# Graph-attention layer front end: norm weight and bias applied as the turned tile leaves PSUM, loads in another order, half of the first accumulator cleared by GpSimd in the front

## The reference

```python
def _gat_conv(x, edge_index, W, att_src, att_dst, bias, heads, out_ch, concat):
    ...
    h = (x @ W).reshape(n, heads, out_ch)
    a_src = jnp.sum(h * att_src[None], axis=-1)
    a_dst = jnp.sum(h * att_dst[None], axis=-1)
    e = jax.nn.leaky_relu(a_src[src] + a_dst[dst], NEG_SLOPE)
    ...
    out = jax.ops.segment_sum(h[src] * alpha[..., None], dst, num_segments=n)
    ...
mu = jnp.mean(x, axis=-1, keepdims=True)
var = jnp.var(x, axis=-1, keepdims=True)
h = (x - mu) / jnp.sqrt(var + LN_EPS) * ln_w + ln_b
h = jax.nn.elu(_gat_conv(h, edge_index, W1, att_src1, att_dst1, b1, H1, C1, True))
return _gat_conv(h, edge_index, W2, att_src2, att_dst2, b2, 1, D, False)
```

## Time and profile before

| | us |
|---|---|
| median of 3 runs | 3159.04 (3158.66 to 3159.12) |
| the profiled execution | 3158.56 |
| its span, first to last instruction | 3156.7 |
| front, to the last `rows` (L519) | 0 to 135.2 |
| first gather of the first walk | 138.86 |
| first walk's gathers | 880, L785, 871.0 busy |
| busy over the span: PE, DVE, POOL, ACT | 2642.0, 2378.1, 1829.8, 1356.0 |

### The profile page before, as it was taken

How to read it: one execution, slowest core, us unless ns; L and a number is a source line. 1 busy time by engine, 2 the same in 40 slices (tenths; PEclk the granted TensorE clock), 3 DMA queues, 4 the chain that set the end, 5 groups by cost and what they waited for, 6 DMA issues and landing times. The chain is left out here.

```text
span 3156.7 us, 72672 instructions
## 1 busy us (share of the span) xinstructions
PE 2642.0 (84%) x16531; PEld 2040.5 (65%) x16532; DVE 2378.1 (75%) x7838; ACT 1356.0 (43%) x5016; POOL 1829.8 (58%) x1892
## 2 busy tenths in 40 slices
PE   6789889888888988796888877877778774999997
PEld 5667767776776777684666665655555554666675
DVE  5699889889988988876777666777888763446465
ACT  3456656665665655342333322444444224221211
POOL 0167777777777777205777777777777735011111
PEclk9889999999999999897999998889989865999999
DMA  6467777777777777214555936333343435232320
GB/s 187 146 195 222 221 215 225 220 223 216 222 222 215 209 209 208 81 56 122 159 154 151 317 106 188 106 106 105 106 106 105 106 106 193 89 102 74 123 73 9
DMA packets 217462, 489.43 MB, mean 155 GB/s; under 512 B 47565, under 2 KB 97241, under 8 KB 217258
## 3 DMA queue, kind: packets, MB, share of 16 engines
q0 software_dynamic: 119696, 367.15, 41.5%
q1 hardware_dynamic: 82782, 106.04, 10.5%
q10 hardware_dynamic: 14780, 13.93, 1.4%
HBM read 427.70 MB, written 64.16 MB: 156 GB/s over the span
## 5 line engine op out<-in xcount | busy, mean ns | idle before, releaser
L1286 POOL DMA_INDIRECT weights<-table,w_idx x880 | 843.1, 958 | 403.9 <-issue 245.6
L785 POOL DMA_INDIRECT w_G<-table,w_idx x880 | 871.0, 990 | 347.8 <-issue 255.6
L918 PE MATMUL PS<-w_G,w_S 128*128 128x260 f32 x3520 | 885.2, 394 | 130.9 <-DVE ACC L1010 112.4
L918 PEld LDWEIGHTS PS<-w_G,w_S 128*128 128x128 f32 x3520 | 637.3, 191 | 236.3 <-issue 86.3
L1493 PE MATMUL PS<-weights 128*128 128x257 f32 x1760 | 530.9, 432 | 141.3 <-DVE ACC L1690 71.8
L1493 PEld LDWEIGHTS PS<-weights 128*128 128x128 f32 x1760 | 336.0, 211 | 251.7 <-issue 154.9
L998 DVE TENSOR_TENSOR w_G<-w_G 128x512 f32<-128x512 f32 x660 | 436.8, 690 | 31.3 <-ACT w_G L815 19.1
L826 ACT ACTIVATE w_G<-w_G 128x64 f32<-128x64 f32 x1760 | 441.3, 335 | 0.0
L1314 ACT ACTIVATE w_PW<-w_Z 128x4 f32<-128x4 f32 x220 | 45.2, 205 | 694.5 <-DVE w_Z L1675 694.3
L1010 DVE TENSOR_TENSOR ACC<-ACC,PS 128x520 f32 x464 | 320.4, 690 | 15.9 <-PE PS L918 15.9
L2397 POOL DMA_INDIRECT out<-Oe,who x64 | 62.3, 973 | 414.8 <-DVEq L2449 408.1
(11 more groups left out here) (333 smaller groups left out, 3799.5 us busy)
## 6 DMA issues: line engine op xcount, KB each, us to landing
xbuf<-XR SPq DMA_DIRECT2D x8, 2064.0 KB
weights<-in_L_ffn_w SPq DMA_DIRECT2D x16, 1024.0 KB, 8.5
XB<-xbuf SPq DMA_DIRECT2D x7, 2064.0 KB, 8.7
w_G<-table,w_idx POOLq DMA_INDIRECT x880
weights<-table,w_idx POOLq DMA_INDIRECT x880
table<-row SPq DMA_DIRECT2D x49, 260.0 KB, 2.0
xw_wide_path<-table SPq DMA_DIRECT2D x49, 260.0 KB, 4.0
table<-row ACTq DMA_DIRECT2D x49, 129.0 KB, 2.2
```

The costliest lines, as they stand in the source:

```text
L785: pool.indirect_dma_start(G[:, r, b, :], None, table, IndexOn(ap=idx[:, r, b:b + 1], axis=0)).then_inc(fetched[r], 16)
L918: last = pe.matmul(PS[:, 2 * j + a, 0:W // layer.banks], lhsT, rhs, start=b == slots[0], stop=b == slots[-1])
L1286: pool.indirect_dma_start(G[:, r, b, :], None, table, IndexOn(ap=idx[:, r, b:b + 1], axis=0)).then_inc(fetched[r], 16)
```

## The change

It does six things.

1. BA, `bias`, its four matmuls and `weights` are gone. `copy(t)` is now two ACTIVATEs of 128x128 (one per half), each with the norm's bias and weight as per-partition operands; it waits once for their load (`norm_in`). `rows(t)` copies instead of adding BA.
2. The two att loads stand on SP's queue behind the first piece of x, and no longer on ACT's behind W1.
3. PIECES are 4, 9, 14 and 22. The first four tiles are normalised, turned and copied ahead of `tile(0)`. `attention` is cut in two, with `scales(0)` between its halves.
4. DVE's side work stands at other tiles: `statistics` of the second piece behind `rows(0)` too, `scales` of the third and fourth piece behind `rows(9)` and `rows(23)`, `crossings` behind `rows(24)` (before, `rows(13)`).
5. xt is no tile of its own. It lies in the part of ACC from tile 24 on, so ACC is there from the front on.
6. POOL clears ACC's tiles 0 to 23 in the front, in one memset behind its two fetches for `crossings`; the memset of DVE in the walk is gone, and ACT clears tiles 24 to 48.

```diff
-PIECES = (4, 13, 16, 16)
+PIECES = (4, 9, 14, 22)
+BLANKED = 24
...
-        xt = sb("xt", [P, TILES, D])
+        xt = ACC[:, BLANKED:, :].rearrange("p t c -> p (t c)")[:, 0:TILES * D].rearrange("p (t d) -> p t d", d=D)
...
             piece(0)
+            for j, v in enumerate((dev["att_s1"], dev["att_d1"])):
+                sp.dma_start(att[:, j, :], v.rearrange("h c -> (h c)").partition_broadcast(P)).then_inc(w1_in, 16)
...
                                         IndexOn(ap=slot_i[:, 0:1], axis=0)).then_inc(across_in, 16)
+            pool.memset(ACC[:, 0:BLANKED, :], 0.0)
...
-                act.activation(YT[:, t % 4, :, :], PS[:, 4 + t % 2, 0:2 * P].rearrange("p (k q) -> p k q", k=2), ACT.Copy).then_inc(y_copied, 1)
+                for k in range(2):
+                    last = act.activation(YT[:, t % 4, k, :], PS[:, 4 + t % 2, k * P:(k + 1) * P], ACT.Identity, bias=lb[:, k:k + 1], scale=lw[:, k:k + 1])
+                last.then_inc(y_copied, 1)
...
-                dve.tensor_tensor(row[:, r, :].rearrange("p (a b) -> p a b", a=2), PS[:, 2 * u:2 * u + 2, 0:HALF],
-                                  BA[:, 0:ROW1].rearrange("p (a b) -> p a b", a=2), ALU.add)
-                dve.tensor_tensor(AD1[:, t, :], PS[:, 2 * u + 1, HALF:HALF + 16], BA[:, ROW1:ROW1 + 16], ALU.add).then_inc(rows_ready, 1)
+                dve.tensor_copy(row[:, r, :].rearrange("p (a b) -> p a b", a=2), PS[:, 2 * u:2 * u + 2, 0:HALF])
+                dve.tensor_copy(AD1[:, t, :], PS[:, 2 * u + 1, HALF:HALF + 16]).then_inc(rows_ready, 1)
...
+            def some(t, first, per, p):
+                a = FROM[p] + per * (t - first)
+                if first <= t and a < FROM[p + 1]:
+                    statistics(p, range(a, min(a + per, FROM[p + 1])))
+
-            statistics(0, range(0, 4))
+            statistics(0, range(0, FROM[1]))
             spread(0)
-            attention()
+            attention(0)
             scales(0)
-            bias()
-            statistics(1, range(4, 17))
-            weights()
+            attention(1)
+            statistics(1, range(FROM[1], FROM[1] + 5))
             for t in range(TILES):
+                if t == 1:
+                    statistics(1, range(FROM[1] + 5, FROM[2]))
+                    spread(1)
                 rows(t)
...
+                some(t, 0, 2, 2)
+                some(t, 10, 2, 3)
+                if t in (7, 21):
+                    spread((7, 21).index(t) + 2)
+                if t in (9, 23):
+                    scales((9, 23).index(t) + 2)
+                if t == 24:
                     crossings()
...
-            dve.memset(ACC[:, 0:HALFWAY, :], 0.0).then_inc(zeroed, 1)
-            dve.wait_ge(zeroed, 1 + -(-(TILES - HALFWAY) // 4))
+            dve.wait_ge(zeroed, -(-(TILES - BLANKED) // 4))
```

More of the change, by code:

```diff
@@ L242, in gps_program @@
             ACC = sb1("ACC1", [P, TILES, ROW1])
+            dev.update(W2A=W2A, b1c=b1c, b1m=b1m, AD1=AD1)
+            front(nc, allocator, dev, ACC)
             walk(nc, allocator, dev, LAYER1, table1, AD1, ADM, SELF, ACC)
@@ L263, in gps_program, with front @@
         return dev
-PIECES = (4, 13, 16, 16)
-def front(nc, allocator, dev):
+PIECES = (4, 9, 14, 22)
+BLANKED = 24
+def front(nc, allocator, dev, ACC):
     PS, ident, iota_row, ones, mean, rstd, unit, SRC, DST, TK, AD1 = (dev[k] for k in (
@@ L388, in copy @@
                     act.wait_ge(tile_done, t - 3)
-                act.activation(YT[:, t % 4, :, :], PS[:, 4 + t % 2, 0:2 * P].rearrange("p (k q) -> p k q", k=2), ACT.Copy).then_inc(y_copied, 1)
+                for k in range(2):
+                    last = act.activation(YT[:, t % 4, k, :], PS[:, 4 + t % 2, k * P:(k + 1) * P], ACT.Identity, bias=lb[:, k:k + 1], scale=lw[:, k:k + 1])
+                last.then_inc(y_copied, 1)
             root(0)
-            normal(0)
-            normal(1)
-            for t in range(TILES):
+            for t in range(FROM[1]):
+                normal(t)
+            act.wait_ge(norm_in, 2 * 16)
+            for t in range(FROM[1]):
+                copy(t)
+            root(1)
+            normal(FROM[1])
+            normal(FROM[1] + 1)
+            for t in range(FROM[1], TILES):
                 if t + 2 < TILES:
@@ L397, in _ @@
                 copy(t)
-                if t in (1, 13, 29):
-                    root((1, 13, 29).index(t) + 1)
+                if t in (10, 24):
+                    root((10, 24).index(t) + 2)
                 if t == 31:
@@ L438, in _ @@
             pe.wait_ge(consts, 4)
[L439 to L445, removed]
+            for t in range(FROM[1]):
+                turn(t)
             pe.wait_ge(wa_ready, 1)
             for t in range(TILES):
-                if t + 2 < TILES:
+                if t >= FROM[1] and t + 2 < TILES:
                     turn(t + 2)
                 tile(t)
+                if t in (FROM[1] - 2, FROM[1] - 1):
+                    turn(t + 2)
                 if t == 5:
@@ L484, in scales @@
                 dve.scalar_tensor_tensor(nmr[:, a:b], mean[:, a:b], -1.0, rstd[:, a:b], ALU.mult, ALU.mult).then_inc(scaled, 1)
[L486 to L510, removed]
+            def attention(k):
+                if k == 0:
+                    dve.wait_ge(w1_in, 6 * 16)
+                cols = WA[:, k, 0:ROW1].rearrange("p (a b) -> p a b", a=2)
+                for j in range(2):
+                    fold_.link(dve.tensor_tensor(prod[:, :].rearrange("p (a b) -> p a b", a=2), cols[:, :, 0:256],
+                                                 att[:, j, :].rearrange("p (a b) -> p a b", a=2), ALU.mult))
+                    fold_.link(dve.tensor_reduce(WA[:, k, ROW1 + 8 * j:ROW1 + 8 * j + 8],
+                                                 prod[:, :].rearrange("p (h c) -> p h c", c=C1), X, ALU.add))
+                last = dve.tensor_copy(cols[:, :, 256:260], WA[:, k, ROW1:ROW1 + 8].rearrange("p (a b) -> p a b", a=2))
+                fold_.link(last)
+                if k == 1:
+                    dve.sem_inc(wa_ready, 1)
@@ L737, in walk @@
         zeroed = sem("x" + tag + "zeroed")
-        HALFWAY = TILES - (28 if H > 1 else 20)
+        assert H > 1
         def nothing(tiles_):
@@ L842, in _ @@
                 stage(n, n)
-            for at in range(HALFWAY, TILES, 4):
+            for at in range(BLANKED, TILES, 4):
                 some = range(at, min(at + 4, TILES))
```

25 lines of the change are left out of this document (2 added, 23 removed).

## The result

| | before | after |
|---|---|---|
| median of 8 runs | 3158.1 (3156.0 to 3159.1) | 3149.5 (3146.2 to 3157.0) |
| the profiled execution | 3158.56 | 3157.04 |
| its span | 3156.7 | 3155.3 |
| start of the last `rows` | 134.56 | 133.23 |
| first gather of the first walk | 138.86 | 137.55 |

The ratio is 0.9975, with an interval from 0.9966 to 0.9985: the medians are 8.6 us apart, where 10.8 were forecast (a time of 3148.2, counted from a median before of 3159.0). The profiled execution of the changed kernel is the slowest of its eight, 7.5 us above their median, so this trace shows where waits went, but its span doesn't show what they are worth.

A forecast was written before the change was run, and what follows sets the result against it. PE was taken to bound the front and POOL's gathers the first walk. Terms -7.8 - 8.1 + 1.6 + 3.5 = -10.8 took 3158.56 to 3147.8, or 3148.2 against the median; range 3142.5 to 3152.5.

The forecast's parts named there:

- the walk's wait: First walk: without DVE's memset POOL's wait for PE's sums falls from 8.07 to 0.30, -7.8 us (bounds 0 and 7.8).
- the start, at `rows(6)`: Front's start: att lands sooner, then rows(4) waits for the store of tile 0; rows(6) at 39.8, not 47.96, -8.1 us.
- scales, twice: Front, tiles 11 and 23: scales one tile nearer its first use makes PE wait 0.8 twice, +1.6 us (0 to 2.4).
- the memset in the front: Front, behind rows(24): POOL's memset holds DVE's casts in edges_to_float until it ends, +3.5 us (bounds 0 and 4.5).
- The 2.22 idle: Walk: DVE's idle time in front of its memset, which may stay with the scaling now there; left in.
- The fallback: Start: if att lands no sooner (13.66), all before is 4 us later, the store's wait hides most, rows(6) at 41.
- the lower bound of 7.3: Start: the smallest gain given at rows(6), -7.3 us, where the forecast was -8.1 and the other bound -11.0.
- the third rival: Front: the memset catches an earlier operation and PE comes back slow after idling, +3 to +4, so 3152; chance 0.10.
- The first gather: Start of the first walk: a sign that the forecast is right, about 3 us sooner, at 135.9.
- The first rival: Front: POOL's memset and DVE's casts don't meet, so the 3.5 is not lost: 3144.7; chance 0.28.
- the second: Walk: POOL's stall stays because its step waits for something the memset hid, +7.8, so 3156.0; chance 0.07.
- The fourth: Walk: more gathers meet DVE casts; one in 15 more adds 17.6 us, 3165.8, slower than before; chance 0.03.

The follow-up runs named there:

- the second profile: The changed kernel measured and profiled again, with no edit: median 3151.4, ratio 0.9978 to the kernel before.
- loads one by one: The change with earlier scales and POOL's memset behind rows(10), W2, att vectors, b1, SE, DE loaded behind tiles 7, 11, 15, 19: 3812.9 (slower chips), 3143.1.
- the late loads: The changed kernel with the six loads between x and the first store issued behind the store of tile 7: 3822.8 against 3826.1 before.
- the earlier scales: The changed kernel with spread, root and scales of the third and fourth piece one tile earlier: 3818.7 against 3826.1 before.

## Why the prediction was right

The time was 1.3 us off, the gain 2.2: 8.6 for 10.8. The time is nearer than the gain because the median of the kernel before came out at 3158.1 and not at 3159.0; that is luck. Term by term, against the two profiles of the change:

| term | forecast | measured |
|---|---|---|
| the walk's wait | -7.8 | -7.6, -7.7 |
| the start, at `rows(6)` | -8.1 | -7.0, -6.8 |
| scales, twice | +1.6 | +1.7, +1.7 |
| the memset in the front | +3.5 | +4.0, +3.2 |
| together | -10.8 | -8.9, -9.6 |

- **The walk** was right in cause and size: POOL asks again without waiting, and putting the memset back brings the wait back (9.6). The 2.22 idle, left in for safety, went too; it made no difference, as POOL set the pace by then.
- **The start**: the step that failed is "Bounds for their landing are 8.33 (no wait) and 13.66 (as before); I take 8.33". The reason looked only at the queue that att had left; W1, on the other queue, landed at 11.31 and became the last. `tile(0)` came at 18.87 instead of 16.2, `rows(3)` at 32.62 instead of 29.0. The store of tile 0, forecast for 37.0, landed at 37.7 and hid most of those 3.6 us, as the prediction said it would. The fallback, `rows(6)` at 41 with att as late as before, was wrong by 2.6: with att landing at 14.30 it was 43.56, a gain of 4.4, so the lower bound of 7.3 was too near. How the rest of the 7 us divides between the folding that is gone, the other pieces of x and the early `scales(0)` was not measured: no run takes one of them out alone.
- **The scales**: the gaps from `rows(10)` to `rows(11)` and from `rows(24)` to `rows(25)` are 2.84 and 2.95 instead of 2.03, so 1.7, and one tile earlier PE's waits are gone.
- **The memset** ran from 82.81 to 93.33, forecast to end near 93.4. What it catches was forecast as a cast in `edges_to_float`; it was the scaling before it, 1.5 us sooner, in `unit_first`. The prediction had this case among its bounds, at 4.5. That is the first half of the third rival. Its second half, PE's slow matmuls, came in the first profile and not in the second, and the 0.8 between 4.0 and 3.2 goes with them. Neither is the 3 to 4 more of that rival: DVE was held 4.7 longer than without the memset, and in the second profile 1.5 of that was PE's slack.
- **The first gather** was forecast for 135.9 and came at 137.6 and 137.0, as the start was worth 1.1 to 1.3 less.
- **The first rival**, no meeting, is out by the 4.91; **the second**, a stall that stays, by the 0.30. **The fourth**, the gathers' pace, did not decide: (busy + idle - the first wait) / 880 gives 1.298 and 1.295, before (its one wait left out) 1.294. The higher 1.298 is mostly the middle gather's 949 ns in place of 946. Those that take over 1.1 us rose from 120 to 128, and to 130 in the second profile, so a few more meetings are in it.
- **The small gain of the first profile.** Its span is only 1.4 shorter, for terms of -8.9. Longer gathers took 3.6 in the first walk, the second walk was 1.3 longer than before the change, the stretch between the walks 1.3, and what stands behind them 1.3. The change touches no code behind the first walk. The stretch behind both walks is 1.9 longer than before in the second profile, too; whether the change does that or executions scatter isn't shown.

The Trainium skill (SBUF — State Buffer, Who interferes with whom) has a VectorE operation in a two-port mode wait for the whole GpSimd instruction. The trace agrees, with 4.91 and the four waits of 1.5 to 1.9, and operations that read PSUM pass, as at `rows` beside the memset. The measurement goes further in one point: six instructions without a gap held DVE as one (5.09).

## What to carry to other kernels

Put a long GpSimd memset where VectorE has no scaling or cast from SBUF to SBUF, the operations that were held here. Look for such a stretch (here moments and copies out of PSUM), and don't cut the memset in pieces instead. When a load is moved forward, ask which load is then the last, on every queue; and when one that nobody needs yet is moved back, give each its own place between the stores. Time won ahead of an operation with a fixed end is worth nothing until that end moves too.

## What was unexpected of the hardware

- Six memsets in a row keep DVE out until the last has ended (5.09 us), 0.2 us between them let it in (1.53, then 0.16 at full speed).
- Even a scaling of 49 columns (0.2 us) and a cast of 4 (1.80) are held, while the two TENSOR_TENSOR of the same 49 columns just ahead pass in 0.20 and 0.21.
- One execution had the gathers of both walks longer (shortest 945 ns against 940 and 942, middle one 949 against 946 and 947). That is worth some 2.6 us in a walk whose pace POOL sets. Whether it goes with the execution or with the chip isn't known, as the chip of that one isn't on record.
- The same program takes 21% longer on two of the four chips. The front is the same there to about a microsecond, but in the first walk POOL's idle time doubles. The group of the gathers in the last version (loads one by one), on the second kind and on the first:

```profile
L781 POOL DMA_INDIRECT w_G<-table,w_idx x880 | 868.2, 987 | 630.1 <-PE PS L914 259.9 <-issue 259.0 <-remote 57.1
```

```profile
L781 POOL DMA_INDIRECT w_G<-table,w_idx x880 | 871.4, 990 | 317.7 <-issue 257.7 <-ACT w_idx L799 51.8 <-PE PS L914 8.2
```

  So the 7.8 us of this change can't simply be carried over to such a chip. With the late loads, whose walk is the changed kernel's, POOL still waits 7.27 us at its first wait for PE's sums, and 1.8 ahead of nearly each block after. The times against the kernel before (0.9993 with the late loads, 0.9981 with the earlier scales) leave open how much is gained there. The changed kernel itself wasn't timed on one. The granted clock of whole executions is 0.85 there and 0.93 on the first kind; whether that is a cause or comes from PE's waiting isn't shown, and the cause of the slowness stays open.
